# A vision tower's step pipeline: the first expert layer in plain fp32 on two halves of TensorE's rows

## The reference

```python
h = patches(x) @ W.T + b                                  # (16, 784, 64)
# recurrent part, over the 16 images, for each token:
xp = layernorm(h) @ W_ih.T + b_ih + b_hh
hid_t = tanh(xp_t + hid_{t-1} @ W_hh.T)
h = h + hid
# mixture of 16 experts, the best 2 of each token:
x2 = layernorm(h)
logits = x2 @ gate_w + gate_b                             # 16 of them
topk_w = softmax(top_2(logits))
hexp = relu(x2 @ w1[e] + b1[e])                           # 64 -> 128, all 16 experts
y_e = hexp @ w2[e] + b2[e]                                # 128 -> 64
moe = sum over the 2 chosen of topk_w * y_e
out = h + layernorm(x2 + moe) * gamma + beta
```

## Time and profile before

| | |
|---|---|
| median of 3 runs | 593.36 us (590.58 to 593.87) |
| the profiled execution | 591.16 us, its span 589.4 us |
| mean granted clock of TensorE | 0.984 of full |
| busy: TensorE, VectorE, ScalarE, GpSimd | 525.7, 458.0, 354.8, 156.6 us |
| first layer, matmuls | 194.7 + 175.2 us in 1024 records |
| second layer, matmuls | 199.5 us in 1024 records |
| relu | 228.0 us in 256 |
| product, sum on VectorE | 149.3 in 256, 117.0 + 17.4 in 112 + 16 |

### The profile page before, as it was taken

How to read it: one execution, slowest core, us unless ns; L and a number is a source line. 1 busy time by engine, 2 the same in 40 slices (tenths; PEclk the granted TensorE clock), 3 DMA queues, 4 the chain that set the end, 5 groups by cost and what they waited for, 6 DMA issues and landing times.

```text
span 589.4 us, 8779 instructions
## 1 busy us (share of the span) xinstructions
PE 525.7 (89%) x3024; PEld 346.8 (59%) x3024; DVE 458.0 (78%) x899; ACT 354.8 (60%) x595; POOL 156.6 (27%) x113
## 2 busy tenths in 40 slices
PE   2465999999999999999999999999999999899981
PEld 2255656666665657566665657666665656565641
DVE  1355797979797897979798897979798897977771
ACT  2235455756757575756757575766767574757561
POOL 3132021323215150323205050322305050221223
PEclk9998899999999999999999999999999999999995
DMA  3303756381918456380918457280917355283701
GB/s 86 86 22 86 156 115 150 72 192 36 232 26 180 98 132 147 75 189 26 232 35 179 98 117 162 58 206 19 220 54 184 96 126 137 62 188 74 178 0 41
DMA packets 30061, 67.33 MB, mean 114 GB/s; under 512 B 6978, under 2 KB 12354, under 8 KB 29890
## 3 DMA queue, kind: packets, MB, share of 16 engines
q1 hardware_dynamic: 30018, 66.78, 49.2%
HBM read 59.54 MB, written 7.23 MB: 113 GB/s over the span
## 4 chain that ended last, share of the span: by engine, by line
PE 43%; DVE 30%; DMA 10%; issue 8%; ACT 6%; SPq 2%; POOL 1%; DVEq 0%; POOLq 0%; ACTq 0%
PE pZ L723 16%; PE pO L736 15%; DMA xcur<-x_in 9%; DVE acc L556 8%; DVE prod L540 7%; ACT hexp L413 3%; DVE cen L465 2%; PE pA L747 2%; DVE total L461 2%; PE pB L644 2%; PE pA L662 1%; PE pB L698 1%; PE pA L654 1%; DVE h L586 1%; DVE hit L495 1%
## 5 line engine op out<-in xcount | busy, mean ns | idle before, releaser
L413 ACT ACTIVATE hexp<-pZ,b1c 128x784 f32<-128x784 f32 x256 | 228.0, 907 | 60.4 <-PE pZ L723 60.2
L540 DVE SCALAR_TENSOR_TENSOR prod<-pO,b2c,spread 128x392 f32<-128x392 f32 x256 | 149.3, 620 | 79.4 <-PE pO L736 79.1
L723 PE MATMUL pZ<-xt,w1hi 128*128 128x392 f32 x512 | 194.7, 380 | 12.0 <-ACT hexp L413 11.9
L736 PE MATMUL pO<-hexp,w2s 128*64 128x392 f32 x1024 | 199.5, 506 | 1.4 <-ACT hexp L413 1.3
L723 PE MATMUL pZ<-xt,w1lo 128*128 128x392 f32 x512 | 175.2, 342 | 0.0
L723 PEld LDWEIGHTS pZ<-xt,w1hi 128*128 128x128 f32 x512 | 97.1, 190 | 73.4 <-issue 41.7
L316 POOL TENSOR_TENSOR inv_std<-var,nhalf 112x7 f32<-112x7 f32 x48 | 80.3, 1688 | 201.7 <-DVE var L470 201.7
L736 PEld LDWEIGHTS pO<-hexp,w2s 128*64 128x64 f32 x1024 | 70.7, 137 | 78.9 <-issue 64.9
L556 DVE TENSOR_TENSOR acc<-acc,prod 128x784 f32<-128x784 f32 x112 | 117.0, 1045 | 0.1
L723 PEld LDWEIGHTS pZ<-xt,w1lo 128*128 128x128 f32 x512 | 97.4, 190 | 0.0
L323 POOL TENSOR_TENSOR h2b<-h2c,bet 112x448 f32<-112x448 f32 x16 | 22.0, 1376 | 168.8 <-DMA h2c<-h_dram 168.8
(11 more groups left out here) (69 smaller groups left out, 426.3 us busy)
## 6 DMA issues: line engine op xcount, KB each, us to landing
spread<-gates_dram SPq DMA_DIRECT2D x128, 392.0 KB, 8.3
xcur<-x_in SPq DMA_DIRECT2D x16, 196.0 KB, 9.6
h_dram<-h SPq DMA_DIRECT2D x16, 196.0 KB, 2.2
h2c<-h_dram SPq DMA_DIRECT2D x16, 196.0 KB, 9.6
out<-yo SPq DMA_DIRECT2D x16, 196.0 KB, 8.9
w1f<-w SPq DMA_DIRECT2D x2, 512.0 KB, 6.0
w2s<-w SPq DMA_DIRECT2D x1, 512.0 KB, 6.9
gates_dram<-gt SPq DMA_DIRECT2D x16, 28.0 KB, 2.0
```

The costliest lines, as they stand in the source:

```text
L413: nc.scalar.activation(hexp[u % RING][:, :].rearrange("p (b c) -> p b c", b=2), halves(pZ[u % 2]), ACT.Relu, bias=b1c[:, u:u + 1])\
L540: nc.vector.scalar_tensor_tensor(out=prod[q % RING][:, b * HALF:(b + 1) * HALF], in0=halves(pO)[:, b, :], scalar=b2c[:, q:q + 1], in1=spre ...
L723: last = nc.tensor.matmul(halves(pZ[e % 2])[:, b, :], w[:, e, :], xt[par][:, b * HALF:(b + 1) * HALF], start=(k == 0), stop=(k == 1))
L736: last = nc.tensor.matmul(halves(pO)[k * D:(k + 1) * D, b, :], w2s[:, e, :], hexp[e % RING][:, b * HALF:(b + 1) * HALF], start=True, stop= ...
```

## The change

The first layer becomes plain fp32. `w1s` holds w1 once: the even expert of each pair on rows 0 to 63, the odd one on rows 64 to 127. x2 is written twice side by side (VectorE writes `x2[:, :, 0, :]`, ScalarE copies it to `x2[:, :, 1, :]`), so that after the turn each half of the rows of `xt` holds the whole x2. `first_layer` now takes a pair: for each half of the tokens one matmul per expert, on its half of the rows, into its own PSUM tensor. It stands in even slots; the second layer of the pair before stays in the odd slot behind it. Semaphores count halves of a pair: `relu_half` on ScalarE does one half of the tokens for both experts, in two instructions of 392 columns, and first and second layer wait by halves.

The logits are plain fp32 matmuls of rows 0 to 63 of `xt` against `gw`. VectorE adds the bias in one operation. The sum over pairs begins with half of `xt`, since both halves hold x2. The splits of w1, of the gates' weights and of x2 into high and low parts are gone.

```diff
-        w1f = sb("w1f", [2 * D, E, F])
-        w1hi = sb("w1hi", [2 * D, E, F], f32r)
-        w1lo = sb("w1lo", [2 * D, E, F], f32r)
-        gwf = sb("gwf", [2 * D, E])
-        gwhl = sb("gwhl", [2 * D, 2 * E], f32r)
+        w1s = sb("w1s", [2 * D, Q, F])
+        gw = sb("gw", [D, E])
...
-                           (rbias[rows, 0:1], b_ih.unsqueeze(1)), (rbias[rows, 1:2], b_hh.unsqueeze(1)),
-                           (gwf[rows, :], gate_w)]
-            expert_loads += [(w1f[rows, :, :], w1)]
-        cell_loads += [(gbias[:, :], gate_b.partition_broadcast(P))]
+                           (rbias[rows, 0:1], b_ih.unsqueeze(1)), (rbias[rows, 1:2], b_hh.unsqueeze(1))]
+            expert_loads += [(w1s[rows, :, :], w1.rearrange("d (q k) f -> k d q f", k=2)[k])]
+        cell_loads += [(gw[:, :], gate_w), (gbias[:, :], gate_b.partition_broadcast(P))]
...
-                if known(t, 0) and gate:
-                    pool.wait_ge(w1_split, 1)
-                    nc.gpsimd.tensor_tensor(w1lo[:, :, :], w1f[:, :, :], w1hi[:, :, :].bitcast(f32), ALU.subtract)\
-                        .then_inc(w1_split, 1)
...
+            def relu_half(t, q, b):
+
+                n = t * Q + q
+                act.wait_ge(z_ready, 2 * n + b + 1)
+                if not known(n, 2):
+                    act.wait_ge(y_ready, 2 * (n - 2) + b + 1)
+                if known(n, 1) and b == 0:
+                    act.wait_ge(experts_loaded, EXPERTS_LOADED)
+                for e in (2 * q, 2 * q + 1):
+                    nc.scalar.activation(hexp[e % RING][:, b * HALF:(b + 1) * HALF], halves(pZ[e % 2])[:, b, :],
+                                         ACT.Relu, bias=b1c[:, e:e + 1]).then_inc(h_ready, 1)
...
-                        nc.scalar.activation(hexp[u % RING][:, :].rearrange("p (b c) -> p b c", b=2),
-                                             halves(pZ[u % 2]), ACT.Relu, bias=b1c[:, u:u + 1])\
-                            .then_inc(h_ready, 1)
+                        relu_half(t, u // 2, u % 2)
...
-                        nc.scalar.activation(x2hl[:, :, 0, :], x2[:, :, :], ACT.Copy).then_inc(MIX.sem, 1)
+                        nc.scalar.activation(x2[:, :, 1, :], x2[:, :, 0, :], ACT.Copy).then_inc(MIX.sem, 1)
...
-                    sofar = xt[par][:, :].bitcast(f32)
+                    nc.vector.scalar_tensor_tensor(out=acc[par][:, :], in0=xt[par][:, :], scalar=0.5,
+                                                   in1=prod[q % RING][:, :], op0=ALU.mult, op1=ALU.add)\
+                        .then_inc(summed, 1)
...
-                    if mix and u == 14:
-                        MIX.wait(dve, s, "hi")
-                        nc.vector.tensor_tensor(x2hl[:, :, 1, :], x2[:, :, :], x2hl[:, :, 0, :].bitcast(f32),
-                                                ALU.subtract).then_inc(MIX.sem, 1)
...
                 for i in range(TILES):
-                    last = nc.tensor.matmul(pB[0:P, i * 2 * E:(i + 1) * 2 * E], xt[par][:, i * P:(i + 1) * P],
-                                            gwhl[:, :], start=True, stop=True)
+                    last = nc.tensor.matmul(pB[0:P, i * E:(i + 1) * E], xt[par][0:D, i * P:(i + 1) * P], gw[:, :],
+                                            start=True, stop=True)
...
                 for b in range(2):
-                    for k, w in enumerate((w1hi, w1lo)):
-                        last = nc.tensor.matmul(halves(pZ[e % 2])[:, b, :], w[:, e, :],
-                                                xt[par][:, b * HALF:(b + 1) * HALF], start=(k == 0), stop=(k == 1))
-                last.then_inc(z_ready, 1)
+                    if not known(n, 1):
+                        pe.wait_ge(h_ready, 4 * (n - 1) + 2 * b + 2)
+                    for k in range(2):
+                        rows = slice(k * D, (k + 1) * D)
+                        last = nc.tensor.matmul(halves(pZ[k])[:, b, :], w1s[rows, q, :],
+                                                xt[par][rows, b * HALF:(b + 1) * HALF], start=True, stop=True)
+                    last.then_inc(z_ready, 1)
...
-                pe.wait_ge(h_ready, 2 * n + 2)
                 for b in range(2):
+                    pe.wait_ge(h_ready, 4 * n + 2 * b + 2)
...
-                    if experts:
-                        first_layer(t, u, par)
+                    if experts and u % 2 == 0:
+                        first_layer(t, u // 2, par)
```

More of the change, by code:

```diff
@@ L24, in vit_tower_kernel @@
     f32 = mybir.dt.float32
-    f32r = mybir.dt.float32r
     i32 = mybir.dt.int32
@@ L102, in vit_tower_kernel @@
         h2 = sb("h2", [P, TILES, D])
-        x2 = sb("x2", [P, TILES, D])
-        x2hl = sb("x2hl", [P, TILES, 2, D], f32r)
-        xt = [sb(f"xt{i}", [2 * D, TOK], f32r) for i in range(2)]
+        x2 = sb("x2", [P, TILES, 2, D])
+        xt = [sb(f"xt{i}", [2 * D, TOK]) for i in range(2)]
         lg = sb("lg", [P, TILES, E])
@@ L139, in vit_tower_kernel @@
         EMBED = Chain("embed_stage", "h1 sum center square var rstd norm turned xn1t_odd xn1t")
-        MIX = Chain("mix_stage", "pre hid_odd hid hid_turned h2_even h2 sum center square var rstd x2 hi lo "
+        MIX = Chain("mix_stage", "pre hid_odd hid hid_turned h2_even h2 sum center square var rstd x2 twice "
                                  "turned_a turned_b xt_a xt_b")
-        GATE = Chain("gate_stage", "logits hi_part biased max1 hit1 ranked1 first1 best1 without "
+        GATE = Chain("gate_stage", "logits biased max1 hit1 ranked1 first1 best1 without "
                                    "max2 hit2 ranked2 first2 best2 diff exp den p1 p2 g1 g2 gates turned gt")
@@ L423, in body @@
                         new_hidden(t + 2)
-                    if known(t, 0) and gate and u == 4:
-                        act.wait_ge(experts_loaded, EXPERTS_LOADED)
-                        nc.scalar.activation(w1hi[:, :, :], w1f[:, :, :], ACT.Copy).then_inc(w1_split, 1)
                     if gate and u == 6:
@@ L482, in bias_logits @@
                 GATE.wait(dve, s, "logits")
[L483 to L487, removed]
+                fresh = pB[0:P, 0:TILES * E].rearrange("p (i e) -> p i e", e=E)
+                nc.vector.tensor_tensor(lg[:, :, :], fresh, over_tiles(gbias[:, :], E), ALU.add).then_inc(GATE.sem, 1)
             def find(s, k):
@@ L551, in add @@
                     MIX.wait(dve, step, "xt_b")
-                    sofar = xt[par][:, :].bitcast(f32)
+                    nc.vector.scalar_tensor_tensor(out=acc[par][:, :], in0=xt[par][:, :], scalar=0.5,
+                                                   in1=prod[q % RING][:, :], op0=ALU.mult, op1=ALU.add)\
+                        .then_inc(summed, 1)
                 else:
                     dve.wait_ge(summed, n)
-                    sofar = acc[par][:, :]
-                nc.vector.tensor_tensor(acc[par][:, :], sofar, prod[q % RING][:, :], ALU.add).then_inc(summed, 1)
+                    nc.vector.tensor_tensor(acc[par][:, :], acc[par][:, :], prod[q % RING][:, :], ALU.add)\
+                        .then_inc(summed, 1)
             def body(t, par, experts=False, gate=False, mix=False, embed=False, close=False):
@@ L605, in body @@
                     if mix and u == 12:
[L606 to L610 removed]
+                        norm_scale(MIX, s, 1, x2[:, :, 0, :])
             embed_sum(0, 0)
@@ L677, in x2_turn @@
             def x2_turn(s):
-                MIX.wait(pe, s, "lo")
+                MIX.wait(pe, s, "twice")
                 if not known(s, 1):
@@ L687, in x2_turn @@
                         last = nc.tensor.transpose(bank[:, (i - first) * P:(i - first + 1) * P],
-                                                   x2hl[:, i, :, :].bitcast(f32).rearrange("p a d -> p (a d)"),
+                                                   x2[:, i, :, :].rearrange("p a d -> p (a d)"),
                                                    ident[0:P, 0:P])
@@ L710, in gates_turn, with first_layer @@
                 last.then_inc(GATE.sem, 1)
-            def first_layer(t, e, par):
-                n = t * E + e
-                if e == 0:
+            def first_layer(t, q, par):
+                n = t * Q + q
+                if q == 0:
                     MIX.wait(pe, t, "xt_b")
                 if known(n, 1):
-                    pe.wait_ge(w1_split, 2)
-                if not known(n, 2):
-                    pe.wait_ge(h_ready, n - 1)
+                    pe.wait_ge(experts_loaded, EXPERTS_LOADED)
                 for b in range(2):
-                    for k, w in enumerate((w1hi, w1lo)):
-                        last = nc.tensor.matmul(halves(pZ[e % 2])[:, b, :], w[:, e, :],
-                                                xt[par][:, b * HALF:(b + 1) * HALF], start=(k == 0), stop=(k == 1))
-                last.then_inc(z_ready, 1)
+                    if not known(n, 1):
[5 more added lines that the diff above has]
+                    last.then_inc(z_ready, 1)
             def second_layer(t, q):
                 n = t * Q + q
```

(2 more changed lines are left out.)

9 lines of the change are left out of this document (removed).

## The result

| | before | after |
|---|---|---|
| median of 6 runs | 590.8 us | 597.94 us |
| the profiled execution, its span | 591.16, 589.4 us | 599.87, 598.1 us |
| ratio of the times, with its 95% interval | | 1.0088 (1.0054 to 1.0121) |

The changed kernel is slower, by 0.9% as the ratio is put and by 1.2% (7.1 us) between the two medians; I had forecast no change. After the three runs shown first, three more of the kernel before came out at 590.6 to 590.8, so its median fell from 593.36 to 590.8.

The account below looks back on a forecast made before the run. No engine alone was taken as the bound, but a chain of waits: VectorE's leg, then TensorE and ScalarE from x2. Span 589.4 + 3.6 (steps) - 3.0 (fill) - 0.7 (tail) = 589.3, forecast as 593.3 us; range 582 to 612.

Parts of the forecast that it names:

- Half relu: ScalarE's relu of 392 elements costs 0.58 us; three split relus between x2 and the next first product add +0.48 a step.
- VectorE's leg: From a step's first product to the write of x2: -0.31 us a step, as one logits operation goes.
- rival C: First layer's two halves by rows do not run together: 2.84 us a pair, 711 us; chance 0.14 with partial overlap.
- Rival B: First layer's weight loads are exposed in each round: +0.33 us a pair, 1.85, time 610 us; chance 0.07.
- Rival A: Split relus cost no more than whole ones and ScalarE stops binding: 586.6 us, 584 with shorter logits; chance 0.31.
- Rival D: Waits put at nothing (copy of xn before the recurrence, pair 4 behind ScalarE) cost 0.4 a step: 599 us; chance 0.14.
- steps of 33.9: Sign to look for: steady steps of 33.9 us from first product to first product, against 33.64 before.
- The rest of that leg: From x2 to the next first product: last half's relu -0.04, first layers -0.57; with relus and logits +0.57 a step.
- the logits' term: Logits on TensorE as fourteen fp32 records for seven f32r matmuls: 1.39 us for 0.70, +0.70 a step.
- The tail: Seven pairs at the end where only TensorE counts, 1.62 to 1.52 us each: -0.7 us.
- what the relu of the last half releases: On TensorE after x2, half a pair (0.87 us) and not one expert (0.91) follows the last relu: -0.04 a step.
- The fill: Before the steady steps: -3.0 us, from -3.15 for cen, -1.30 for x2's low part, -0.84, +2.8 for logits, -0.5.

Follow-up runs that it names:

- run 1: The kernel before with each relu split into two instructions of 392 columns, nothing else: 598.31 us, 1.0112 of the kernel before.
- run 4: The changed kernel with the logits on all 128 rows, `gw` zero in its lower 64: 595.41 us, 1.0068 of the kernel before.
- run 3: The changed kernel without halves by rows in the first layer: w1 in both halves, products on 128 rows, relu scaled by a half: 717.43 us, a single run.
- run 6: The changed kernel with the close's seven scalings on ScalarE one slot later, behind the last half's relu: 589.83 us, 0.9958 of the kernel before.
- the three kernels that show it: The changed kernel, run 4 and run 5: VectorE's leg of step 13 is 21.16, 21.14 and 21.12 us, with the lower clock there.
- run 5: The changed kernel with one GpSimd tensor_tensor of 128x2048 put back in the fill, on its own tile: 600.17 us, 1.0112 of the kernel before.

## Why the prediction was wrong

**Right, to a few hundredths.** The pair's first layer: 1.52 forecast, 1.518 measured. Half relu 0.58 (0.582), +0.48 for three (0.44 ahead of the turn of x2 in run 1). VectorE's leg -0.31 (-0.3). First layer without concurrency 2.84 (2.78 to 2.83), rival C's time 711 (717.43): its mechanism did not occur, its price was right. Rival B did not occur either: the rounds inside a pair follow each other by 0.33 as in the second layer, and the pair keeps to 1.52. Rival A fell with run 1. Rival D's figure, 599 us, is nearest to the measured time, but by luck: its places, the copy of xn and pair 4, are not where the time is. The sign "steps of 33.9" also came near by luck. The 33.64 it was added to is one of the longest steps of before, most of which take 32.9 to 33.1; those of the changed kernel take 33.57 where nothing disturbs them, and 33.82 on the mean.

**The step that failed** is "The rest of that leg" with the logits' term. I had +0.48 - 0.04 - 0.57 + 0.70 = +0.57 and measured +0.93. The first two came to +0.38. The others, +0.13 in the forecast, came to +0.55: the logits +0.78, 0.08 over the forecast +0.70; the turn of x2, which I priced at nothing since it isn't edited, +0.16; the turn of xn likewise, +0.18. Run 4 shows 0.18 of these 0.42 to be the logits' use of half the rows. Run 3 shows 0.09 of the turn of x2 to come from the first layer's use of half the rows behind a turn on all of them, and 0.05 of the turn of xn from the half rows of the first layer ahead of it. The rest of both turns, 0.07 and 0.04, goes with fp32 and not f32r following. Why that costs is open. Over the 14 legs the forecast was +8.0 us and the traces have +12.4, so 4.4 us are from here (the first leg grew by 0.54 only, the last by 0.85).

A change from the whole array to half the rows costs TensorE 0.09 us ahead of its first matmul in these runs, and at the logits as much again behind it (run 4). The change brought new ones: from the turn of x2, of the sum, from the embedding to a first layer (1.43 for 1.34 in run 3), from the turn of xn to the logits. The Trainium skill (TensorEngine Tiling (Array Packing), Key Properties) says that changing the tiling mode drains TensorE. The trace agrees, with 0.09 us and with a first load that passes no earlier than its matmul, and I did not weigh the rule.

**The tail** was forecast at -0.7 and is +0.7, another 1.4. Seven pairs did get shorter. But in the last step the scalings stand ahead of the last half's relu, and that is now half of a pair, so the second layer of the last half waits for it. Run 6, with the scalings behind that relu, has 60.6 us in this stretch for 62.1. The chain at the end:

```profile
578.25 1.66 ACT yn L373 x7
579.91 0.95 ACT hexp L402 x2
...
580.90 0.90 PE pO L715 x4
```

The step "what the relu of the last half releases" was applied to the steady step only.

**The fill** gave 1.1 more than forecast. The second logits took 1.48 us, 0.33 more than the 1.15 of before, and not 1.4 more as I had. The granted clock goes with it. Windows of the kernel before and of the changed one, between x2 and the first product:

```profile
55.30:61.00 5.70, 5.70 (x23) 4.83 (x25) 0.00 (x0) 3.06 (x5) 0.00 (x0) 0.50 1.02 231
```

```profile
54.00:60.00 6.00, 6.00 (x40) 3.99 (x38) 1.66 (x4) 3.52 (x8) 0.00 (x0) 1.00 1.02 228
```

Before, the turn of xn, a first layer, the logits, the recurrence and the second layer went at the lower level there. In the changed kernel the first pair still took 2.92 us, from 51.44, though its rows give a granted clock of 1.00; what followed the turn of xn ran at full pace. I forecast with the old pace and did not ask what the change would do to the clock.

**The VectorE leg** was forecast at -0.31 a step and is that on the mean of twelve steps (-0.33), but not in two: step 3, whose patches landed late (2.4 us), and step 13, where the granted clock fell behind TensorE's wait for ScalarE (1.6 us over the forecast). No term of the prediction has the clock in the steps. That the change brings the fall in step 13 is argued from the three kernels that show it and from the kernel before and run 6, which don't; what sets it off is open.

In all, from 589.3 forecast to 598.1: 8.8 = 4.4 (legs) + 1.4 (tail) - 1.1 (fill) + 2.4 (step 3) + 1.6 (step 13) + 0.1 left over.

The account of the change in the steady step is thus: split relus with the shorter last half +0.38, logits +0.78 less 0.31 on VectorE, the two turns +0.34, first layers and the wait for xt -0.57: +0.62, where I had +0.26. The missing low part and 16 us less on VectorE are not in it, because they did not stand on the path.

## What to carry to other kernels

Price what an edit does to the unedited neighbours on the same engine: a tiling or a number format is a property of a sequence, and its changes cost where it meets another. Splitting an instruction costs its fixed part again, and where that engine's queue stands ahead of the path the sum is paid in full; look there for a piece that can stand one place later, which here gave back more than the change had lost. And before a wait is subtracted, add up the busy slots of the engine that released it: they are a floor, if not always what the step ends on.

## What the runs showed of the hardware

- Plain fp32 on two halves of the rows runs at 1.8 times the pace of all rows: 1.52 for 2.78 to 2.83 us, four products of 392 columns (run 3).
- Whole array to half the rows: 0.09 us ahead of the first matmul at each change, and 0.09 more behind it at the small fp32 matmuls of 112x16: fourteen records, 1.48 for 1.39, all but the first 0.10 apart in both (run 4).
- A VectorE operation of 0.63 us took 3.47 beside a GpSimd tensor_tensor of 3.60, and ended 0.5 after it (run 5).
- The granted clock was 0.51 from 164 to 167, after TensorE had idled 0.92 us before 162.59, and 0.50 from 509 to 512, after 1.53 us of idle. Idle alone does not tell: in the kernel before TensorE idles 0.93 us in a step (before 314.46) and 1.48 in step 13 with the clock at 1.00.
